# A convolution, scan and expert block on one core: the order of the first fourteen microseconds

## What is computed

```python
def _forward(x, in_proj_w, conv_w, conv_b, xproj_w, dt_w, ...):   # x is group-normed
    xz = x @ in_proj_w
    xi, z = jnp.split(xz, 2, axis=-1)
    xc = conv_general_dilated(xi as NCHW, conv_w, (1, 1), ((1, 1), (1, 1)))   # 3x3
    xc = silu(xc + conv_b)                       # "u" in the kernel
    x_dbl = einsum('bchw,oc->bohw', xc, xproj_w)
    ...
    delta = softplus(einsum('kbrl,kdr->kbdl', dt_stack, dt_w) + dt_b)
    ys = vmap(_selective_scan)(xs, delta, A, Bst, Cst, Ds)   # 4 directions, 16 states each
    ...
x = x + layer(_gn(x));  t = t + attention(_ln(t));  t = t + experts(_ln(t))
```

## Time and profile before

| | us |
|---|---|
| median of 3 runs | 200.75 |
| lowest and highest | 200.68, 201.4 |
| span of the profiled execution | 199.8 |
| median over that span | 0.95 |
| TensorE, VectorE, ScalarE, GpSimd busy | 189.0, 154.2, 138.2, 101.5 |

### The profile page before, as it was taken

How to read it: one execution, slowest core, us unless ns; L and a number is a source line. 1 busy time by engine, 2 the same in 40 slices (tenths; PEclk the granted TensorE clock), 3 DMA queues, 4 the chain that set the end, 5 groups by cost and what they waited for, 6 DMA issues and landing times.

```text
span 199.8 us, 2692 instructions
## 1 busy us (share of the span) xinstructions
PE 189.0 (95%) x771; PEld 86.9 (43%) x773; DVE 154.2 (77%) x257; ACT 138.2 (69%) x286; POOL 101.5 (51%) x121
## 2 busy tenths in 40 slices
PE   7799999799999998999899999989999999999993
PEld 2334654344545534455345455836333333233231
DVE  6486899999999999999989954757676553945652
ACT  2629896999999999989989914555853452443430
POOL 7676668698899859999799900000000224000000
PEclk9999999999999999999999999999999999999999
DMA  4699543437958669683967200000000443000000
GB/s 148 143 240 176 167 159 110 144 125 219 270 187 215 185 170 289 226 211 118 310 205 234 73 0 0 3 0 0 0 0 7 126 102 74 17 3 0 0 0 26
DMA packets 20941, 23.38 MB, mean 117 GB/s; under 512 B 7897, under 2 KB 12478, under 8 KB 20926
## 3 DMA queue, kind: packets, MB, share of 16 engines
q1 hardware_dynamic: 20750, 23.11, 41.0%
q10 hardware_dynamic: 176, 0.10, 0.2%
HBM read 22.92 MB, written 0.28 MB: 116 GB/s over the span
## 4 chain that ended last, share of the span: by engine, by line
PE 48%; DMA 12%; DVE 7%; POOL 5%; issue 5%; SPq 0%; DVEq 0%; POOLq 0%
PE ps L1204 20%; PE ps L1224 10%; PE ps L986 8%; DMA cr<-c_rows 6%; DMA c_rows<-cb 6%; POOL rings L439 5%; DVE rings L717 4%; PE ps L993 2%; PE ps L909 1%; DVE ps L707 1%; PE ps L1154 1%; PE ps L1234 1%; PE ps L1173 1%; PE ps L1262 1%; PE ps L1074 1%
## 5 line engine op out<-in xcount | busy, mean ns | idle before, releaser
L439 POOL TENSOR_TENSOR rings<-rings,cr 128x512 f32<-128x512 f32 x59 | 73.4, 1270 | 10.4 <-DVE rings L717 4.7
L717 DVE TENSOR_TENSOR_SCAN rings<-rings,ps 128x512 f32<-128x512 f32 x64 | 74.3, 1200 | 0.6 <-ACT rings L536 0.4
L613 ACT ACTIVATE si<-ps 128x512 f32<-128x512 f32 (+1 forms) x44 | 26.3, 597 | 31.2 <-PE ps L1204 30.8
L886 DVE TENSOR_TENSOR rings<-ps,si 128x512 f32<-128x512 f32 (+1 forms) x42 | 28.8, 689 | 23.8 <-ACT si L613 23.3
L536 ACT ACTIVATE rings<-delta,a_neg 128x510 f32<-128x510 f32 x64 | 43.5, 707 | 0.0
L1204 PE MATMUL ps<-fd,wup 64*128 64x512 f32 (+1 forms) x136 | 41.3, 606 | 0.6 <-DVE fd L819 0.5
L517 ACT ACTIVATE scaled<-du_tok,b_tok 128x128 f32<-128x128 f32 x116 | 36.7, 387 | 0.7 <-PE ps L993 0.6
L986 PE MATMUL ps<-rings,ident 128*128 128x512 f32 x64 | 33.1, 599 | 1.8 <-POOL rings L439 1.8
L986 PE MATMUL ps<-rings,flip 128*128 128x512 f32 x64 | 32.3, 598 | 0.7 <-POOL rings L439 0.7
L461 POOL TENSOR_TENSOR fdg<-fd,gb 64x512 f32<-64x512 f32 x4 | 5.0, 1268 | 49.7 <-DMA gb<-g_rows 49.7
L1204 PEld LDWEIGHTS ps<-fd,wup 64*128 64x128 f32 (+1 forms) x136 | 15.7, 182 | 23.7 <-issue 12.4
(11 more groups left out here) (215 smaller groups left out, 179.2 us busy)
## 6 DMA issues: line engine op xcount, KB each, us to landing
cr<-c_rows SPq DMA_DIRECT2D x60, 256.0 KB, 3.8
wup<-w_up_dram SPq DMA_DIRECT2D x8, 341.0 KB, 5.8
wdn<-w_down_dram SPq DMA_DIRECT2D x4, 160.0 KB
wdn<-w_down_dram SPq DMA_DIRECT2D x4, 128.0 KB
gb<-g_rows SPq DMA_DIRECT2D x4, 128.0 KB, 4.7
delta<-g_rows SPq DMA_DIRECT2D x4, 128.0 KB, 3.7
w_conv<-conv_w_dram SPq DMA_DIRECT2D x1, 384.0 KB, 4.8
gmap<-g_rows SPq DMA_DIRECT2D x2, 172.0 KB
```

The source lines that it names most:

```text
L439: nc.gpsimd.tensor_tensor(hc[:, q], hs[:, q], cr[:, row_slot(n)] if n >= ROWS_FROM else cs[:, q], ALU.mult).then_inc(weighted, 1)
L613: nc.scalar.activation(si[0:rows, S % 2, :], ps[0:rows, BANK_H + 2 * (S % 3), :], ACT.Silu).then_inc(silu_ready, 1)
L717: nc.vector.tensor_tensor_scan(hs[:, q, :], da[:, q].rearrange("p b l -> p (b l)"), driven(q), 0.0, ALU.mult, ALU.add).then_inc(scanned, 1)
L886: nc.vector.tensor_tensor(gated[0:rows, S % GATED, :], linear, si[0:rows, S % 2, :], ALU.mult).then_inc(glu_ready, 1)
```

## The change

Four edits, all in the head. The second copy of x is issued by ScalarE, between its two other issues, and no longer by SP. On TensorE the first column product stands ahead of the second fold, the other two behind it, and the delta merge `combine(0)` behind those. On VectorE `keep_comb(0)` stands behind the four `d_cross` instructions. The single tap's product reads all 128 partitions; a memset on VectorE makes the lower half of its weights zero, with a semaphore for it.

```diff
@@ sync @@
             sp.dma_start(w_xp[:], xproj).then_inc(xp_in, 16)
-            sp.dma_start(xc[C:2 * C, 0:T], x_chan).then_inc(xc_in, 16)
             sp.dma_start(by_tap[:, :, 2], conv_by_tap[:, :, 2]).then_inc(conv2_in, 16)
@@ scalar @@
             act.dma_start(w_in[:], in_proj).then_inc(win_in, 16)
+            act.wait_ge(edge_zero, 2)
+            act.dma_start(xc[C:2 * C, 0:T], x_chan).then_inc(xc_in, 16)
             act.wait_ge(dt_zero, 1)
@@ vector @@
             nc.vector.memset(w_dt[:], 0.0).then_inc(dt_zero, 1)
+            nc.vector.memset(w_fold[C:2 * C, FOLD_PAIRS + 1], 0.0).then_inc(fold_zero, 1)
...
-            dve.wait_ge(comb_ready, 1)
-            keep_comb(0)
-
             dve.wait_ge(prm_in, PRM_IN)
             dve.wait_ge(pool_step, 8)
             for half in range(K // 2):
...
+            dve.wait_ge(comb_ready, 1)
+            keep_comb(0)
@@ tensor @@
+            def column_pair(y):
+                nc.tensor.matmul(ps[:, 2, :], w_fold[:, y, :], x_col[:, :, y:y + H, 0:W], start=(y == 0), stop=False)
+
+            pe.wait_ge(xn_ready, B)
+            pe.wait_ge(fold_kept, 1)
+            column_pair(0)
             pe.wait_ge(conv2_in, 16)
             fold(BANKS_FOLD[1], 0, slice(2, TAPS, 6), 2)
             fold(BANKS_FOLD[1], 1, slice(5, 6), 1).then_inc(fold_ready, 1)
+            column_pair(1)
+            column_pair(2)
             pe.wait_ge(dt_in, 32)
             pe.wait_ge(xpT_kept, 1)
             combine(0)
-
-            pe.wait_ge(xn_ready, B)
-            pe.wait_ge(fold_kept, 1)
-            for y in range(FOLD_PAIRS):
-                nc.tensor.matmul(ps[:, 2, :], w_fold[:, y, :], x_col[:, :, y:y + H, 0:W], start=(y == 0), stop=False)
             pe.wait_ge(fold_kept, 3)
-            nc.tensor.matmul(ps[:, 2, :], w_fold[0:C, FOLD_PAIRS + 1, :], x_col[0:C, :, 2:2 + H, 2:2 + W], start=False, stop=False)
+            pe.wait_ge(fold_zero, 1)
+            nc.tensor.matmul(ps[:, 2, :], w_fold[:, FOLD_PAIRS + 1, :], x_col[:, :, 2:2 + H, 2:2 + W], start=False, stop=False)
```

More of the change, by code:

```diff
@@ L196, in hybrid_kernel @@
         pad_zero = sem("pad_zero")
+        fold_zero = sem("fold_zero")
         xp_in, dt_in = sem("xp_in"), sem("dt_in")
```

## The result

| us | kernel before | changed kernel |
|---|---|---|
| executions | 20 | 20 |
| median | 200.72 | 202.43 |
| lowest, highest | 199.97, 204.68 | 200.55, 203.83 |
| mean | 201.58 | 202.32 |
| ratio, 95% interval | | 1.0068 [1.0043, 1.0094] |

The account below looks back on a forecast made before the run. TensorE was taken to bound the head, VectorE the scan loop. First product at 8.03 us plus 6.07 us of TensorE work ended at 14.10 instead of 14.27: gain 0.17, so 200.75 became 200.6 us; range 199.7 to 201.4.

Parts of the forecast that it names:

- The bound: Head: TensorE has no gap from 8.19 to 14.27 us; an earlier copy gains only what TensorE can start before 8.19.
- Part 1: Head DMA: second copy of x issued on ScalarE's queue at 1.41 us, landing with the first copy or before.
- d: Head DMA: later landing of first weights, first copy and `w_xp` through the moved copy; 0.27 us, between 0 and 0.55.
- Cost 0: ScalarE's queue: the new issue of 0.5 to 0.6 us fits a 0.6 us hole; bound 0.1 us, absorbed by slack.
- Part 2: TensorE in the head: first column product ahead of the second fold, merge later; splitting the column products adds 0.19 us.
- T0: TensorE in the head: start of the first column product, after first fold, transposes and image; claimed 8.03 us.
- rival A: TensorE and DMA: cheaper shape changes or free DMA share, 0.3 us each, both together 200.1 us; chance 0.20.
- Part 3: TensorE in the head: single tap in 128 rows, one shape with the row product; -0.20 us, its memset hidden.
- Part 4: VectorE in the head: `keep_comb(0)` behind the four `d_cross` instructions; cost 0 with 0.9 us to spare.
- B: DMA engines, 3 to 6.5 us: the copy starves the first weights, loss of 0.1 us, 200.9 us; chance 0.12.
- C: Scan loop: C-row writes fall into another rhythm; half either way 199.6 or 201.7 us, whole 198.7 or 202.5; chance 0.18.
- The offset: Whole kernel: median taken as 0.95 us above the profiled span, kept for the forecast.

Follow-up runs that it names:

- fill: Changed kernel with two more idle products on TensorE between the statistics' product and the first fold: median 202.05 us, ratio 1.0035.
- tap_fill4: Kernel before with the 128-partition tap, idle products in TensorE's three head waits and a fourth ahead of the statistics' product: median 201.09 us, ratio 1.0001.
- look2: Changed kernel, no edit, one more profiled execution: 200.41 us, `u` starting at 14.38 us.
- again: Changed kernel repeated without edit, 12 executions: median 202.55 us, ratio 1.0092; its profiled execution took 203.95 us.
- after_fill2: Changed kernel with idle products added: four before the first fold, one before the transposes, one before the first column product: median 201.36 us, ratio 0.9994.
- look3: Changed kernel, no edit, another profiled execution: 202.44 us at a mean clock of 0.99, `u` starting at 16.39 us.
- tap_again: Kernel before with only the single tap in 128 partitions and its weights' memset, repeated: median 200.26 us, ratio 0.9975.
- order_tap_fill: Kernel before with the 128-partition tap, filled waits and the new order of products, merge and `keep_comb(0)`, copy on SP: median 202.94 us, ratio 1.0089.
- look1: Changed kernel, no edit, one more profiled execution: 203.26 us at a mean clock of 0.998, `u` starting at 17.23 us.
- less_warm: Kernel before without the three idle products between the projection's transpose and the statistics' product: median 203.79 us, ratio 1.0113.
- before_fill: Kernel before with idle products added: three before the first fold, one before the transposes, one before the second fold: median 201.04 us, ratio 1.0000.
- tap_fill: Kernel before with the single tap in 128 partitions and idle products added in TensorE's three head waits: median 200.95 us, ratio 1.0016.

## Why the prediction was wrong, point by point

**The bound.** Right that the head's end is TensorE's and that an early copy is worth only what TensorE can start before 8.19 us. Right too that all behind `u` shifts as a block, at least until 64 us.

**Part 1, the term d.** Mis-sized, by its own steps. d = 0.27 us was the middle between 0 and 0.55; it came out as 0.6 (first weights 5.4 us to landing against 4.8) and 0.5 (`w_xp`), at the bound of 0.55. SP's own copy was hit hardest, 1.1 us, which no term held: I gave it the same d. In the traces other than those of `fill` and `tap_fill4`, whose idle products are in its way longest, the first fold starts at 6.22 to 6.80 us with the copy on SP (8 traces) and at 6.45 to 7.36 with it on ScalarE (8). The landing also scatters by itself: the first weights take 4.1 to 5.3 us with the copy on SP and 4.9 to 5.8 with it on ScalarE. One execution, `look2`, had nearly no delay and was as fast as before. The second weights, which were to land at 8.1 us as before, landed at 3.39 + 4.9 = 8.3 us, and nothing waited for them. The free share of the engines ahead of 3.5 us didn't take the copy: moved earlier it met the 384 KB. The rule of the Trainium skill that the prediction drew on (DMA: Bandwidth & Descriptors, "Issuing engines are not separate DMA queues") fits this: another issuer gave the copy no way of its own.

**Part 1, ScalarE.** Cost 0 failed by a little: the issue took 0.85 us and not 0.5 to 0.6, the table load began at 3.67 instead of 3.31 us, and `sd_g` came 0.17 us later. With the idle products at 1.2 GHz until 5.6 us, the copy to `mr_c` ended at 6.54 us and not at 6.11.

**Part 2, T0 and the sum.** T0 was to be 8.03 us and is 8.63 us. The first fold was kept at 8.42 us and the transposes done at 8.25, but the image, which was to be 0.27 us early, came last: written from 7.48 (not 6.62) for 1.1 us, to 8.58. So the wait that ended last was again that for a copy of x, now SP's. The sum from T0 was 6.07 us and measured 14.72 - 8.63 = 6.09. The weight loads of the second fold (9.69) and of the next column product (10.26) start with their own products, so a product of 128*128 beside one of 128*64 does hold the load back. The row that was missing is there now, and it agrees with what the Trainium skill says of changes of tiling mode (TensorEngine Tiling (Array Packing), "Key Properties"); rival A's 0.3 us isn't to be had.

**Part 3** was right in size, 0.2 us inside the change and 0.40 us alone, and it is the only part that pays.

**Part 4** was right: `keep_comb(0)` ended at 13.88 us, the second merge started at 14.96.

**The rivals.** B has the right place (weights starved by the copy) and d above its threshold of 0.43; by its price it gives 200.9 us, a loss of 0.1, and at d = 0.6 with the image late it was 0.46. C's spread is real but isn't shown to be the change's: the second half of the loop varies by up to 1.8 us across the 18 traces, by 0.2 us in the five of the changed kernel, while the time from `u` to the third write varies by 0.13 us at most. It doesn't explain the shift of the executions. (By C's own price, half of 1.9 us on top of 200.6 is 201.5 or 201.6 us, not the 201.7 of the prediction.)

**The step that failed** is one that the prediction took without a reason: that TensorE runs through the head at 2.4 GHz. All terms of its sum (1.05, 0.57, 1.92, 0.62, 1.91 us) are durations of one execution at that clock, and a wait of TensorE was priced as its length only. Forecast was a gain of 0.17 us; the terms of part 1 and T0 turn that into a loss of 0.46 us, and the rest of the 1.7 us in the median goes with the clock, as far as the filled runs show it (202.55 us in `again`, 201.36 in `after_fill2`). The trace of before had the warning in it: its three idle products, each 512 columns,

```profile
4.23 0.88 PE L909 MATMUL ps<-warm 128*128 128x512 bf16 x3
```

took 0.88 us together, less than the 1.46 us of later traces: the clock had risen only then, at about 4.5 us, with waits of 0.42 us to come at 6.3 and 8.2 us. The price of one fallen clock is read from `look3`: `u` 1.56 us later than in the first profile. The changed kernel has such a mean clock in 13 of 35 executions, the kernel before in none of 117, and the added idle products take it away. The price of a rise only behind 12.5 us, from `again`, is 2.9 us, but executions above 203 us are about as frequent before the change (30%) as behind it (34%), so that kind isn't what the change brought.

What in the change makes the clock fall is known less well. It isn't the sum of TensorE's waits: from the statistics' product to the first column product these are 0.42 + 0.17 + 0.42 us in the trace of before and 0.69 + 0.38 us in that of the change. Nor is it the longest wait alone. `tap_again` waits longer than either and keeps 2.4 GHz:

```profile
6.80 0.87 PE L927 MATMUL ps<-w_conv,w_inT 128*64 128x384 f32 x4 [0.91 <-DMA w_conv<-conv_w_dram]
7.89 0.39 PE L940 MATMUL ps<-ident,w_xp 128*32 128x128 f32 x2 [0.22 <-DMA w_xp<-xproj_dram]
8.74 0.65 PE L927 MATMUL ps<-w_conv,w_inT 128*64 128x256 f32 x4 [0.46 <-DMA w_conv<-conv_w_dram]
```

**The offset.** The median was taken as 0.95 us above the span. An execution's own time is 1.74 or 1.75 us above its span (200.94 and 199.2, 203.95 and 202.2). By that the profiled execution of before took about 201.5 us (an estimate: 199.8 + 1.74), with 1.1 us of loop above the least. The offset hid that the profile was no median one.

**What stays open.** Why two in ten of the changed kernel's executions still escape, since nothing in a trace shows what decides in one execution when the clock rises or falls; where the low stretch lies at a mean clock of 0.983, of which no trace was caught; what makes the loop's second half vary; why `order_tap_fill` is slow without a low clock; and why part 3 and the fills don't add up.

## What to carry to other kernels

Look at all executions before pricing a tenth of a microsecond: where they fall in groups 1.5 and 3 us apart, a change is worth what it does to the shares of the groups. In a kernel's head, before TensorE's clock is steady, read the clock from the pace of like products, count each wait of TensorE that a change moves or lengthens as a risk of microseconds, and try the change with its waits filled by idle products as well. Of the parts of this change the one that shortens TensorE's work paid, and those that move work did not. A DMA that is issued earlier into full engines delays what it joins, and the one that suffers most may be the one its user also waits for.

## What the runs showed of the hardware

- The granted clock of the trace says 1.00 from the start although the idle products run at half pace: `again` has 1.00 in every stage of its head, 0.998 over the span, and 1.2 GHz until past 12.5 us by the pace of its products (first fold 1.55 us, 0.87 at 2.4 GHz). A fall after a rise is recorded (0.50 in `look3`), a rise that hasn't come yet is not, in the traces of `again`, `look1` and `less_warm`.
- Three idle products of 512 columns ahead of 6 us decide 2.9 us: without them the lowest of six executions is 203.24 us, with them the lowest of 29 is 200.37 (`less_warm`).
- With more idle products in the waits of the head no execution has a low mean clock: 0 of 72 in six runs (`before_fill`, `after_fill2` and the four `tap_fill` runs), against 13 of 35 of the changed kernel.
- A product of 512 columns in fp32 costs 1.05 us between others of another shape and 0.86 us between its likes; two changes of shape less are 0.40 us (`tap_again`: 4.49 us against 4.89).
- Two transfers of 128 KB on two queues: the one issued 0.67 us earlier landed 1.3 us earlier (6.1 and 7.4 us), and the later one took 5.3 us where it had taken 4.2.
